# Attention pairs of a graph layer: every pair's probabilities turned by DMA as two 16-bit planes and multiplied as they are, with the values in three bf16 parts, one step later

## The reference

```python
q, k, v = x @ wq.T + bq, x @ wk.T + bk, x @ wv.T + bv
q2 = (q @ wiq.T + biq).reshape(N, H, D).transpose(1, 0, 2)     # and k2, v2 likewise
scores = jnp.einsum('hnd,hmd->hnm', q2, k2) * scale + mask[None]   # mask from 6144 edges
attn = jax.nn.softmax(scores, axis=-1)
out = jnp.einsum('hnm,hmd->hnd', attn, v2).transpose(1, 0, 2).reshape(N, OUT_F)
return layernorm(x + out @ wo.T + bo)
```

## Time and profile before

| | |
|---|---|
| runs | 293.78 us median, 293.52 to 294.85 (3 runs) |
| the profiled execution | 293.82 us, of which its span 292.1 us |
| PE / DVE / ACT / POOL busy | 284.8 / 193.5 / 160.6 / 134.0 us |
| granted clock | 0.995 of full over the span |
| HBM traffic | 136 GB/s over the span |

### The profile page before, as it was taken

How to read it: one execution, slowest core, us unless ns; L and a number is a source line. 1 busy time by engine, 2 the same in 40 slices (tenths; PEclk the granted TensorE clock), 3 DMA queues, 4 the chain that set the end, 5 groups by cost and what they waited for, 6 DMA issues and landing times.

```text
span 292.1 us, 5219 instructions
## 1 busy us (share of the span) xinstructions
PE 284.8 (98%) x1656; PEld 264.9 (91%) x1656; DVE 193.5 (66%) x486; ACT 160.6 (55%) x310; POOL 134.0 (46%) x114
## 2 busy tenths in 40 slices
PE   8999999999999999999999999999999999999991
PEld 8999999999999998888999999999999999787881
DVE  4889967566766674325157778787878687884085
ACT  5954423442344242421077777777777777697323
POOL 2000745645455542665855344545453535919400
PEclk9999999999999999999999999999999999999998
DMA  7959864463564439845120304030303121555013
GB/s 268 325 186 370 255 203 152 144 212 89 202 217 124 124 117 338 309 144 155 72 68 13 137 7 139 12 132 14 130 19 125 38 105 40 177 91 144 2 72 144
DMA packets 18766, 41.01 MB, mean 140 GB/s; under 512 B 7904, under 2 KB 8768, under 8 KB 18624
## 3 DMA queue, kind: packets, MB, share of 16 engines
q1 hardware_dynamic: 16640, 39.37, 40.9%
q0 software_dynamic: 1680, 0.62, 1.1%
q10 hardware_dynamic: 432, 0.85, 0.8%
HBM read 37.44 MB, written 2.21 MB: 136 GB/s over the span
## 4 chain that ended last, share of the span: by engine, by line
PE 91%; DVE 4%; POOL 1%; ACT 1%; issue 1%; POOLq 0%; DVEq 0%; ACTq 0%
PE bank L983 20%; PE bank L974 18%; PE bank L976 17%; PE bank L975 17%; PE bank L1090 5%; PE bank L1060 5%; PE bank L1072 4%; PE bank L999 3%; DVE stats L948 1%; PE bank L992 1%; POOL w_lo L351 1%; DVE res L947 1%; DVE shared L821 0%; ACT w_hi L433 0%; ACT shared L519 0%
## 5 line engine op out<-in xcount | busy, mean ns | idle before, releaser
L379 POOL DMA_INDIRECT mask_cells<-scratch x48 | 53.9, 1123 | 74.2 <-DMA mask_cells<-scratch 31.8
L351 POOL TENSOR_TENSOR w_lo<-w_raw,w_hi 128x1024 fp32r<-128x1024 f32 x18 | 42.9, 2403 | 47.7 <-DVE shared L832 43.0
L433 ACT ACTIVATE w_hi<-w_raw 128x1024 fp32r<-128x1024 f32 x49 | 51.3, 1053 | 19.4 <-PE bank L983 18.1
L974 PE MATMUL bank<-x_hi,w_hi 128*128 128x384 f32 x176 | 58.8, 334 | 0.0
L975 PE MATMUL bank<-x_lo,w_hi 128*128 128x384 f32 x176 | 58.8, 334 | 0.0
L976 PE MATMUL bank<-x_hi,w_lo 128*128 128x384 f32 x176 | 58.8, 334 | 0.0
L651 DVE TENSOR_TENSOR w_lo<-w_raw,w_hi 128x1024 fp32r<-128x1024 f32 x31 | 38.0, 1227 | 16.5 <-ACT w_hi L433 15.6
L974 PE MATMUL bank<-h_hi,w_hi 128*128 128x384 f32 x128 | 47.2, 369 | 0.0
L476 ACT ACTIVATE h_hi<-bank,bcol 128x384 f32 (+1 forms) x24 | 14.0, 582 | 55.1 <-PE bank L976 49.9
L976 PE MATMUL bank<-h_hi,w_lo 128*128 128x384 f32 x128 | 43.1, 337 | 0.0
L975 PE MATMUL bank<-h_lo,w_hi 128*128 128x384 f32 x128 | 42.9, 335 | 0.0
(11 more groups left out here) (107 smaller groups left out, 522.1 us busy)
## 6 DMA issues: line engine op xcount, KB each, us to landing
w_raw<-weights SPq DMA_DIRECT2D x53, 512.0 KB
shared<-key_rows SPq DMA_DIRECT2D x6, 512.0 KB
shared<-start SPq DMA_DIRECT2D x5, 320.0 KB, 5.9
res<-x_rows SPq DMA_DIRECT2D x1, 1536.0 KB, 6.9
out<-res SPq DMA_DIRECT2D x6, 256.0 KB, 2.0
mask_cells<-scratch POOLq DMA_INDIRECT x48
shared<-start ACTq DMA_DIRECT2D x2, 320.0 KB, 5.2
mask_cells<-mask SPq DMA_DIRECT2D x1, 576.0 KB, 6.1
```

Of the source, the lines that this page charges most:

```text
L351: nc.gpsimd.tensor_tensor(lo, w_raw[:, s, cols], hi.bitcast(F32), ALU.subtract)\
L379: nc.gpsimd.indirect_dma_start(out=mask_cells, out_offset=bass.IndirectOffsetOnAxis(ap=cell[:, c:c + 1], axis=0), in_=cell_value[:, c:c + ...
L433: nc.scalar.activation(w_part(t, s, slice(0, F))[0], w_raw[:, s, :], ACT.Copy).then_inc(w_hi_done, 1)
L974: pe.matmul(out_ps, w_hi[:, s, cols], moving_hi, start=(k == 0), stop=False)
```

## The change

All eight pairs take the way of the last one, and the copies behind the turning fall away:

- `transposes`, `normalise`, `pt_high`, `pt_low`, `turned_high` and `turned_low` are gone. ACT writes six high planes and DVE six low planes for each pair; SP issues four transposes for each pair (`turn(a, h)`), behind the load of tile 41 + 2a. Turned planes of a pair go into one buffer (`turned_hi`, `turned_lo`), so that `turn(a, h)` waits for the value products of pair a - 1 (`pv_done`).
- The low planes lie in the first halves of the places of `probs` (before: in `v2`), so that `mask_scores` of the next pair waits at its places 0 and 3 for the low plane to have landed, and ACT's first high plane of each half for the turned high plane.
- `values` reads the fp16 planes directly. Values are split into three bf16 parts: `v_high` on ACT, and on POOL the rest, its middle and its low part (`v_low`, five instructions in place of three).
- A value group holds both heads: six products of 384 columns for each m, 18 for a pair (12 before). They stand in step a + 2 at k = 5, 6, 7 of the q projection, after that step's scores, and write banks 2 and 4, so that they wait for the masks of places 0 to 2 (banks 0, 2 and 4) of the pair whose scores were just made.
- The two weight splits stand before the softmax on ACT, POOL does the weight low parts before `v_low` and no longer waits for the normalised banks; `att_half_out` and `add_halves` of both heads follow the q evacuation.
- The output projection is put in another order: `values(6)` and `values(7)` (18 products each) lie in it, and behind the last product of node block 0 there is one k of block 1 in place of two.

```diff
-            def transposes(a, g):
-                h, m = divmod(g, NT)
-                pe.wait_ge(probs_ready, 2 * NT * a + NT * (h + 1))
...
+            def values(a, par, m):
+                if m == 0:
+                    pe.wait_ge(vp_done, a + 1)
+                    if isinstance(a, int) and a == PAIRS - 1:
+                        pe.wait_ge(sum_done, 2 * a)
+                    else:
+                        pe.wait_ge(masked, 2 * NT * a + 3 * NT)
+                    for h in range(2):
+                        pe.wait_ge(turned_hi_landed[h], 16 * a + 16)
+                        pe.wait_ge(turned_lo_landed[h], 16 * a + 16)
+                def product(h, cols, turned, start=False, stop=False):
+                    return pe.matmul(out_bank[h][0:cols.stop - cols.start, 0:N].rearrange("p (b q) -> p b q", b=NT),
+                                     vp[:, par, m, h, cols], turned[:, h, :, m, :], start=start, stop=stop)
+                two, low = slice(0, 2 * D), slice(2 * D, 3 * D)
+                for h in range(2):
+                    product(h, two, turned_hi, start=(m == 0))
+                for h in range(2):
+                    product(h, low, turned_hi)
+                for h in range(2):
+                    ins = product(h, two, turned_lo, stop=(m == NT - 1))
...
+            def turn(a, h):
+                if a:
+                    sp.wait_ge(pv_done, NT * a)
+                sp.wait_ge(plane_hi_done, 2 * NT * a + NT * (h + 1))
                 sp.dma_start_transpose(...turned_hi[:, h]..., plane_hi[:, h]...).then_inc(turned_hi_landed[h], 16)
+                sp.wait_ge(plane_lo_done, 2 * NT * a + NT * (h + 1))
                 sp.dma_start_transpose(...turned_lo[:, h]..., plane_lo[h]...).then_inc(turned_lo_landed[h], 16)
...
+            def softmax(a):                     # ScalarE
+                exps(a, range(0, 4))
+                high_planes(a, (0,))
+                exps(a, (4,))
+                high_planes(a, (1,))
+                exps(a, (5,))
+                high_planes(a, range(2, 6))
...
+            def attention(a):                   # VectorE
+                for place in range(5):
                     mask_scores(a, place)
+                invert(a, 0)
                 mask_scores(a, 5)
+                low_planes(a, (0, 1))
+                invert(a, 1)
+                low_planes(a, range(2, 6))
...
             def step(j, par):                   # TensorE, after each k
+                        if which == 0 and k == SCORE_PLACE:
+                            pe.wait_ge(acc_free, L1_TILES + 2 + 2 * j)
...
+                            scores(a, 1 - par)
+                        if which == 0 and more and k >= VALUES_FROM:
+                            values(j - 2, par, k - VALUES_FROM)
```

More of the change, by code:

```diff
@@ L47 @@
 SCORE_PLACE = 3
-TRANSPOSES_FROM, VALUES_FROM = 2, 5
+VALUES_FROM = 5
 LEAD = 2
@@ L541, in turned_high @@
-            def turned_high(groups):
-                for g in groups:
-                    h, m = divmod(g, NT)
[L545 to L549, removed]
+                    nc.scalar.activation(probs[:, place, :], probs[:, place, :], ACT.Exp,
+                                         bias=neg_max[:, place:place + 1], scale=-1.0,
+                                         accum_out=row_sum[:, place:place + 1]).then_inc(exp_done, 1)
@@ new lines, in high_planes @@
+            def high_planes(a, places):
+                for place in places:
+                    h, b = divmod(place, NT)
+                    if b == 0:
+                        if not (isinstance(a, int) and a == 0):
+                            act.wait_ge(turned_hi_landed[h], 16 * a)
+                        act.wait_ge(inv_ready, 2 * a + (h + 1))
+                    nc.scalar.activation(plane_hi[:, h, b, :], probs[:, place, :], ACT.Copy,
+                                         scale=row_inv[:, place:place + 1]).then_inc(plane_hi_done, 1)
@@ L556, in step @@
                 attend = not (isinstance(j, int) and j < 1)
+                more = not (isinstance(j, int) and j < 2)
                 split(t + LEAD, s0, raws)
@@ L561, in step @@
                         act.wait_ge(v2_ready, 2 * NT)
-                    if not (isinstance(j, int) and j < 2):
-                        att_half_out(a - 1, 1)
                     v_high(a, 1 - par)
[L565 to L568, removed]
+                split(t + LEAD + 1, s0 + 1, raws)
+                if attend:
+                    softmax(a)
                 evacuate(t, L1_TILES + 2 * j, par, 0)
[L570 to L575, removed]
+                if more:
+                    for h in range(2):
+                        att_half_out(j - 2, h)
+                    att_high(j - 2)
                 evacuate(t + 1, L1_TILES + 1 + 2 * j, par, 1)
[L577 to L580, removed]
             step(0, 0)
@@ L590, in _ @@
             a = PAIRS - 1
-            att_half_out(a - 1, 1)
             split(WO_TILE + 2, 2, (WO_TILE + 2) // RING + 1)
+            v_high(a, 1)
             split(WO_TILE + 3, 3, (WO_TILE + 3) // RING + 1)
[L594 to L602, removed]
+            softmax(a)
+            for h in range(2):
+                att_half_out(a - 1, h)
             act.wait_ge(tile_done, WO_TILE)
@@ L607, in _ @@
                     att_high(a - 1)
[L608 to L614, removed]
                 high_part(LAST_TILES + i, i, LAST_TILES // RING + 1)
+            for h in range(2):
+                att_half_out(a, h)
+            att_high(a)
             for n in range(NT):
@@ L798, in evacuate_pair, with add_halves @@
                     op0=ALU.add, op1=ALU.subtract).then_inc(acc_free, 1)
-            def add_halves(a, h, scale=None):
+            def add_halves(a, h):
                 dve.wait_ge(half_done, 2 * a + (h + 1))
-                if h == 0 and not (isinstance(a, int) and a == 0):
-                    dve.wait_ge(att_lo_done, a)
+                if h == 0:
+                    dve.wait_ge(att_lo_done, a + 1)
                 here = slice(h * D, (h + 1) * D)
[L807 to L813, removed]
+                nc.vector.scalar_tensor_tensor(out=att_sum[here, :], in0=out_bank[h][here, 0:N], scalar=1.0 / UP,
+                                               in1=att_half[here, :], op0=ALU.mult, op1=ALU.add)\
+                    .then_inc(sum_done, 1)
@@ L815, in mask_scores @@
             def mask_scores(a, place):
                 i = ROW_TILES[place]
+                if place % NT == 0 and not (isinstance(a, int) and a == 0):
+                    dve.wait_ge(turned_lo_landed[place // NT], 16 * a)
                 dve.wait_ge(scores_ready, 2 * NT * a + (i + 1))
                 dve.sem_inc(scores_seen, 1)
-                nc.vector.tensor_tensor_reduce(out=probs[:, i, :], in0=score_bank[i][:, 0:N], in1=mask[:, i // 2, :],
-                                               scale=-SCALE, scalar=3.0e38, op0=ALU.add, op1=ALU.min,
-                                               accum_out=neg_max[:, i:i + 1]).then_inc(masked, 1)
@@ L835, in pt_low @@
[L835 to L848 removed]
+                nc.vector.tensor_tensor_reduce(out=probs[:, place, :], in0=score_bank[i][:, 0:N],
+                                               in1=mask[:, i // 2, :], scale=-SCALE, scalar=3.0e38, op0=ALU.add,
+                                               op1=ALU.min, accum_out=neg_max[:, place:place + 1]).then_inc(masked, 1)
@@ L899, in step @@
                 a = j - 1
-                s0 = (2 * par + LEAD) % RING
-                attend = not (isinstance(j, int) and j < 1)
-                if attend:
-                    attention(a, L1_TILES + 2 * j, par)
-                    pt_low(a, (4, 5))
+                more = not (isinstance(j, int) and j < 2)
+                if isinstance(j, int) and j < 1:
+                    evacuate_pair(L1_TILES + 2 * j, par, 0)
                 else:
+                    attention(a)
                     evacuate_pair(L1_TILES + 2 * j, par, 0)
+                if more:
+                    for h in range(2):
+                        add_halves(j - 2, h)
                 evacuate_pair(L1_TILES + 1 + 2 * j, par, 1)
-                if attend:
-                    add_halves(a, 0)
             SOFTMAX_STEPS = 4
@@ L922, in _ @@
             a = PAIRS - 1
[L923 to L939 removed]
+            attention(a)
+            for pair in (a - 1, a):
+                for h in range(2):
+                    add_halves(pair, h)
             for n in range(NT):
@@ L1156, in _ @@
             project(0, 0, left)
-            for g in range(KT - VALUES_FROM, 2 * NT):
-                values(a - 1, 0, g)
             project(0, 1, left)
@@ L1191, in _ @@
                 project(2, k, slice(1, 3))
-            for k in range(6, KT):
-                last = project(0, k)
-            for ins in last:
+            for ins in project(0, KT - 1):
                 ins.then_inc(y_ready, 1)
-            for k in range(6, KT):
-                last = project(1, k)
```

(2 more changed lines are left out.)

243 lines of the change are left out of this document (70 added, 173 removed).

## The result

The changed kernel takes 302.16 us (median of 4 runs, 300.74 to 303.9), the kernel before beside it 294.0 (4 runs, 293.52 to 294.85): a ratio of 1.0277, with a 95% interval from 1.0218 to 1.0337. I had forecast 290.6, faster, and the range ended at 296.5. From here on, lines without another name are those of the changed kernel.

What follows compares the result with a forecast made beforehand. PE, busy without a gap, bounds the kernel; afterwards the DVE and ACT loop ties with it at 13.4 us. -8.8 before the last scores, +4.2 behind, +1.4 at the end: 293.8 - 3.2 = 290.6 us, range 288.0 to 296.5.

Steps and rivals of the forecast that it cites:

- An inversion takes 0.49: Softmax on DVE: an inversion takes 0.49 us, so the first high plane can start 4.2 us after the first score product.
- what hides it is the 6 us and more that are left: POOL's two added instructions, about 1 to 2 us a step, are hidden by its idle time.
- S1 to S2, 11.1: First score products of steps 1 and 2 stand 11.1 us apart, 0.8 later than PE could.
- Value products at 0.173: On PE, each 16-bit value product of 384 columns costs 0.173 us, like the 4-byte one; bounds 0.160 and 0.32.
- columns only: Rival: 16-bit products cost 0.160 us for 0.173, -0.5 to -1.9, 288.7 to 290.1 us; chance 0.15.
- S2 to S3, 14.1: First score products of steps 2 and 3 stand 14.1 us apart, with 0.7 added for a late turned plane.
- The loop, 13.4: From scores through DVE and ACT to the next scores takes 13.4 us, tying with PE's 13.4.
- The halves: Within a step, two half copies priced like q's evacuation, 0.46 us, and two `add_halves` at 0.6 each.
- The transposes: Four on SP at 1.35 us issue each, landing 3.2 to 4.6 later; in time by 0.3 to 1.7 us, except step 2.
- Behind S8, +4.2: After the last pair's first score product, 36 value products replace 12 on PE: +4.2 us.
- the end, +1.4: First layer norm sum comes 1.36 us nearer to PE's end, so the kernel ends that much further behind: +1.4 us.
- The loop is longer than walked: Rival: DVE and ACT loop 0.7 us longer in each of six periods, +4.2, 294.8 us; chance 0.25.

Runs made afterwards that it cites:

- e3: Changed kernel with row sums scaled on ACT and POOL's value parts started behind the low planes: 295.41 us, ratio 1.0077 to the kernel before.
- e8: On top of e5: q evacuated earlier in step 1, k evacuated before `att_high` on ACT, output block 0 finished earlier: 287.49 us, ratio 0.9772.
- e2: Changed kernel with POOL's `v_low` waiting for the low planes, inversion left as it is: 299.85 us, ratio 1.0207 to the kernel before.
- e4: Changed kernel with POOL's weight low parts waiting for the first inversion: 322.97 us (one run).
- e5: On top of e3, 64 columns of zeros beside the low value part, so every value weight is 128 wide: 292.29 us, ratio 0.9910.
- e7: On top of e3, the value products' moving operand in one piece of 384 columns, giving another output: 296.85 us (one run).

## Why the prediction was wrong, point by point

- **"An inversion takes 0.49", and of POOL "what hides it is the 6 us and more that are left": wrong, and the step that failed.** I priced POOL's move by its idle time and asked only what waits for POOL through semaphores. In its new place its work holds DVE: 1.42 for 0.15 at the first inversion, 1.33 for 0.62 at a low plane. Taking both away (e3) shortens S1 to S8 from 103.35 to 96.11 us, 7.2 of the 11.15; 1.3 of these 7.2 are products at the lower clock in step 1 (next point), so 5.9 are the hold itself.
- **S1 to S2, 11.1: wrong by 3.9.** e3 has 12.83. 0.8 of the 3.9 is the same cause, a gap of 3.04 in place of 2.26. 1.3 more are nine products at the lower clock, which e3's profiled execution didn't have; that the hold brought them on is not shown (last section). The rest, 1.7, is an error in my walk: I ended it at the evacuation of k and overlooked PE's own work between the two evacuations. PE may not begin the next q projection until q is out, and four k of it, 12 x 0.173 = 2.1 us, lie before the next scores. e8 moves the evacuation of q forward and gets 11.07.
- **Value products at 0.173: wrong, 0.203.** On 18 of a step that is 0.54, which is what parts e3's 13.95 from my 13.4. In the changed kernel it is hidden in the steps where the loop is longer still (14.9) and costs from S8 on. My range for one product went up to 0.32, so it held the price; but I set the rival "columns only" (0.160) and the forecast (0.173) against each other by data type, and the cause is the order of the widths. With one width the columns-only rival is right: 0.162 inside a group.
- **S2 to S3, 14.1: near (14.36), but not for my reason.** I had added 0.7 for a late turned plane; none was late, since step 1 took longer, and in e3 PE's own work filled 13.95.
- **The loop, 13.4: right where it could be seen** (13.43 in e3). The halves, priced by neighbours, stand as priced: two `add_halves` in 1.13, two half copies in 1.00.
- **The transposes: right.** SP's lines show issues of 1.25 to 1.72 us and landings 3.3 to 3.9 us after. PE and DVE never wait for them; only in e8, where step 2 begins as early as I had forecast, does one come late.
- **Behind S8, +4.2, and the end, +1.4: right, the first in part by luck.** S8 to PE's end is 41.0 us for 40.65. The 36 value products there cost 1.3 more than I priced (18 in one go take 3.77 in e3, for 3.11), so about 1.0 was saved elsewhere in the stretch; no run shows where. The first layer norm sum comes at 285.70 and the span ends 14.5 us later, PE's last product ends 7.4 before the span's end, for 6.0 before:

```profile
285.70 0.69 DVE L875 TENSOR_TENSOR res<-bank,res 128x512 f32<-128x512 f32 x1 [10.58 <-PE bank L911]
...
292.56 0.28 PE L911 MATMUL bank<-h_hi,x_lo 128*128 128x256 f32 x1
```

- **The rivals.** "The loop is longer than walked" is what happened, and I gave it 0.25 with 294.8 us: I let it be 0.7 longer and it was 1.5, since I looked for the excess in handovers and half copies and not in an inversion priced at 0.49 that took 1.72. The hold also lengthens step 1, by 0.8, where I had let a longer loop cost nothing.
- **The books.** At S8: 5.9 (POOL over DVE) + 1.3 (the lower clock in step 1) + 1.7 (PE's work between two evacuations, step 1) + 2.2 (value products) = 11.1 of 11.15. The 2.2 and 1.7 are read in e3 and e8; in the changed kernel itself the first hides most of the last, so that undoing the value products' part alone there would give little; this was not tried.

## What to carry to other kernels

When work is moved on GpSimd or VectorE, lay it beside the other engine's instructions in the new place and look for those with two SBUF inputs, however small, and for those like L848, held here with one: one of 0.15 us in a chain costs what is left of the GpSimd instruction. In a trace, compare minimum and maximum of one instruction form; a ratio of ten is a lead, and here it stood in the trace of the kernel before (0.15 and 2.23 for its inversion). Keep the weights of consecutive 16-bit products at one width, and pad if need be. And when a loop over several engines is walked, close it at every engine: the work that PE has between two waits belongs to it.

## What the runs showed of the hardware that was not expected

- A 128x3 multiplication on VectorE took 0.15 to 1.45 us in one kernel (1.84 in e2), where it was held ending within 0.02 us of GpSimd's instruction; in e4 two low planes took 4.81 for 1.24.
- 16-bit products of 384 columns stand 0.162 us apart at one weight width, and each change between 128 and 64 columns adds 0.11.
- Near the end of PE's pause of 3.04 us the granted clock fell to the lower of its two levels, 1.2 GHz: the stretch 148.50:163.47 has 0.89, and nine products stand 0.32 us apart, 384 columns at that clock, before the distance is 0.17 again. Behind e3's pause of 2.26 us at the same place they stood 0.17 to 0.29 apart from the first on. The length of the pause doesn't tell the two apart: in the profiled executions of e5 and e7 the clock fell behind a pause of 2.26 us too (S1 to S2 is 14.39 in both, for 12.83 in e3), and behind 2.42 in e2 it didn't. So 1.3 to 1.6 us of a kernel's time depend on the execution, and what decides it stays open.

```profile
160.31 0.52 PE L903 MATMUL bank<-h_lo,w_hi 128*128 128x384 f32 x1
160.63 0.52 PE L904 MATMUL bank<-h_hi,w_lo 128*128 128x384 f32 x1
...
163.04 0.34 PE L903 MATMUL bank<-h_lo,w_hi 128*128 128x384 f32 x1
163.21 0.33 PE L904 MATMUL bank<-h_hi,w_lo 128*128 128x384 f32 x1
```

From e3, and from e5 with the same pause, the step with that pause:

```profile
159.12 0.45 PE L912 MATMUL bank<-h_hi,w_hi 128*128 128x384 f32 x1 [2.26 <-DVE h_lo L786]
148.58:161.41 12.83, 10.57 (x68) 9.75 (x67) 8.07 (x22) 11.31 (x26) 6.93 (x7) 1.00 0.69 182
...
160.87 0.48 PE L913 MATMUL bank<-h_hi,w_hi 128*128 128x384 f32 x1 [2.26 <-DVE h_lo L787]
150.32:164.71 14.39, 12.13 (x67) 11.20 (x66) 8.07 (x22) 11.31 (x26) 8.48 (x8) 0.88 0.75 187
```
